# Post-norm attention with routed experts on one core: the transposed z moved between two projections, weight rounding and four orders moved

## The reference

```python
q, k, v = x@Wq + bq, x@Wk + bk, x@Wv + bv          # 16 heads of 64
attn = softmax(causal(q k^T / 8)); a = (attn v) @ Wo + bo
x = layernorm(x + a)
xn = layernorm(x) * gamma + beta
w, idx = top_k(softmax(xn @ router^T / 1.5), 2)    # 8 experts
y = sum_k w_k * (silu(xn @ W1[idx_k]) @ W2[idx_k])  # hidden 512
x = layernorm(x + y)
```

## Time and profile before

| | |
|---|---|
| median of 3 runs | 1347.1 us (1345.36 to 1347.86) |
| the profiled execution: time, span | 1345.8 us, 1344.0 us |
| TensorE, matmul | 1297.7 us busy, 97% |
| VectorE | 1116.6 us, 83% |
| ScalarE | 1037.2 us, 77% |
| GpSimd | 491.7 us, 37% |
| steps of attention | until about 1021 us |
| expert steps | until about 1296 us |
| last stage | until 1344 us |

### The profile page before, as it was taken

One profiled execution on the slowest core, in us unless ns is written; L12 is line 12 of the kernel. 1 busy time (PEld: TensorE's weight loads), 2 busy tenths in 40 slices (PEclk: granted clock), 3 DMA queues, 4 the chain that ended last, 5 costly groups with the idle time before them and its releaser, 6 DMA issues.

```text
span 1344.0 us, 35085 instructions
## 1 busy us (share of the span) xinstructions
PE 1297.7 (97%) x10918; PEld 1134.5 (84%) x10918; DVE 1116.6 (83%) x5412; ACT 1037.2 (77%) x3402; POOL 491.7 (37%) x1067
## 2 busy tenths in 40 slices
PE   6999999999999999999999999999998999999967
PEld 5888888888888888888888888888887999999953
DVE  6888888888888888888888888888886898888847
ACT  7888888888888888888888888888884555555527
POOL 1023333333333333333333333333335665555545
PEclk9999999999999999999999999999999999999989
DMA  2000000000000000000000000000033777666638
GB/s 82 2 5 17 16 16 19 13 14 13 14 13 13 14 14 14 13 14 18 16 18 15 14 13 14 13 14 14 14 140 114 216 221 219 213 214 209 205 123 327
DMA packets 67641, 89.74 MB, mean 67 GB/s; under 512 B 10352, under 2 KB 37107, under 8 KB 67456
## 3 DMA queue, kind: packets, MB, share of 16 engines
q1 hardware_dynamic: 57808, 70.28, 16.6%
q0 software_dynamic: 8640, 17.13, 3.8%
q10 hardware_dynamic: 1008, 0.08, 0.1%
HBM read 61.66 MB, written 26.71 MB: 66 GB/s over the span
## 4 chain that ended last, share of the span: by engine, by line
PE 93%; ACT 2%; DVE 2%; issue 1%; DMA 1%; POOL 0%; ACTq 0%; POOLq 0%; SPq 0%; DVEq 0%
PE ps_f L1036 15%; PE ps_b L1070 14%; PE ps_a L1036 13%; PE ps_s L1077 12%; PE ps_s L1058 10%; PE ps_s L1235 9%; PE ps_b L1244 5%; PE ps_a L1244 5%; PE ps_s L1061 4%; PE ps_s L1311 2%; PE ps_a L1226 1%; ACT probs L574 1%; PE ps_f L1102 1%; PE ps_s L1082 1%; ACT probs L576 1%
## 5 line engine op out<-in xcount | busy, mean ns | idle before, releaser
L574 ACT ACTIVATE probs<-probs,neg_max 128x256 f32<-128x256 f32 x512 | 255.3, 499 | 127.8 <-DVE neg_max L790 125.4
L786 DVE CUSTOM_DVE_ANT_0 probs<-ps_s,mask 128x256 f32<-128x256 f32 x512 | 214.4, 419 | 37.1 <-PE ps_s L1061 34.3
L450 POOL TENSOR_SCALAR ln_b<-mv 128x2 f32<-128x2 f32 x32 | 6.1, 190 | 637.4 <-DVE mv L853 637.4
L1070 PE MATMUL ps_b<-pt,f_y 128*64 128x256 f32 (+1 forms) x2048 | 196.0, 333 | 10.3 <-ACT f_y L569 7.3
L660 ACT ACTIVATE m_tanh<-ps_s 128x256 f32<-128x256 f32 x284 | 108.8, 384 | 124.7 <-PE ps_s L1235 114.8
L1077 PE MATMUL ps_s<-ident,probs 128*128 128x128 f32 x1536 | 204.7, 274 | 0.0
L576 ACT ACTIVATE probs<-probs,neg_max 128x128 f32<-128x128 f32 x512 | 198.7, 388 | 0.0
L800 DVE TENSOR_SCALAR probs<-probs,inv_sums 128x256 f32<-128x256 f32 x512 | 180.8, 353 | 9.1
L1070 PEld LDWEIGHTS ps_b<-pt,f_y 128*64 128x64 f32 x2048 | 132.0, 137 | 61.0 <-issue 16.3
L540 POOL DMA_INDIRECT y_tok<-m_y,m_dest x142 | 139.7, 984 | 111.5 <-DVE m_dest L946 79.4
L1058 PE MATMUL ps_s<-qk 64*128 64x256 f32 x1024 | 171.3, 408 | 7.9 <-ACT pt L605 1.7
(11 more groups left out here) (193 smaller groups left out, 2988.5 us busy)
## 6 DMA issues: line engine op xcount, KB each, us to landing
m_w<-in_w SPq DMA_DIRECT2D x142, 256.0 KB
m_x<-queue SPq DMA_DIRECT2D x71, 133.0 KB, 3.0
f_y<-y_tok SPq DMA_DIRECT2D x32, 256.0 KB, 6.5
queue<-empty SPq DMA_DIRECT2D x8, 532.0 KB, 5.0
x_raw<-in_x SPq DMA_DIRECT2D x32, 128.0 KB, 2.1
out_x<-f_y SPq DMA_DIRECT2D x16, 256.0 KB, 5.7
y_tok<-m_y,m_dest POOLq DMA_INDIRECT x142
queue<-z,slot_now POOLq DMA_INDIRECT x128, 2.4
```

Of the source, the lines that this page charges most:

```text
L574: act.activation(row[:, 0:2 * P], row[:, 0:2 * P], ACT.Exp, scale=-1.0, bias=neg_max[:, pair, h, 0:1], accum_out=sums[:, d % 2, pair, h, 0:1])
L786: dve.tensor_tensor_reduce(out=row[:, 0:2 * P], in0=ps_s[:, pair, h, 0:2 * P], in1=mask[:].rearrange("p a b -> p (a b)"), scale=-1.0, scal ...
L1070: ins = pe.matmul(ps_b[r, cols], v[:, k, c * P + h * DH:c * P + (h + 1) * DH], pt[:, pair, h, src], start=(k == 0), stop=(k == 1), skip_gr ...
```

## The change

The text of the change, with some unchanged lines left out:

```diff
@@ ScalarE, the start
-            for half in range(2):
+            def round_weights(half, i):
                 cols = slice(half * 512, (half + 1) * 512)
-                for i in range(3):
-                    act.wait_ge(attn_w_loaded[half * 3 + i], 16)
-                    act.activation(wqkv_hi[:, i, cols], wqkv_raw[:, i, cols], ACT.Copy, scale=SCALE if i == 0 else 1.0
-                                   ).then_inc(attn_w_hi, 1)
+                act.wait_ge(attn_w_loaded[half * 3 + i], 16)
+                act.activation(wqkv_hi[:, i, cols], wqkv_raw[:, i, cols], ACT.Copy, scale=SCALE if i == 0 else 1.0
+                               ).then_inc(attn_w_hi, 1)
+
+            for i in range(3):
+                round_weights(0, i)
             act.wait_ge(small_loaded, 16 * 7)
             act.wait_ge(biases_ready, 1)
             evacuate_qk(0, 0)
             evacuate_qk(0, 1)
+            for i in range(3):
+                round_weights(1, i)
@@ ScalarE, a step
+                if q == 3 and n in MID:
+                    act.wait_ge(zt_ready, n)
+                    act.activation(xnt[:].rearrange("p (i t) -> p i t", i=TILES), ps_s[:, 1, :, 3 * P:4 * P],
+                                   ACT.Identity, scale=gamma_sb[:, 0:1], bias=beta_sb[:, 0:1]).then_inc(xnt_done, 1)
                 if d >= 2 and q == 0:
                     copy_outputs(d)
                 if d + 1 < LAST:
                     evacuate_qk(d + 1, 0)
-                if q == 3 and n in MID:
-                    act.wait_ge(zt_ready, n)
                 if 1 <= d <= LAST:
                     first_pt(d)
-                if q == 3 and n in MID:
-                    act.activation(xnt[:].rearrange("p (i t) -> p i t", i=TILES), ps_s[:, 0, :, 3 * P:4 * P],
-                                   ACT.Identity, scale=gamma_sb[:, 0:1], bias=beta_sb[:, 0:1]).then_inc(xnt_done, 1)
@@ VectorE, the start
             rest_of_weights(0, 2)
-            for i in range(3):
-                rest_of_weights(1, i)
@@ VectorE, first_table: parts 4, 5, 6, 7 are now parts 3, 4, 5, 6
@@ VectorE, a step
-                if n == SEQS - 1 and q == 3:
-                    first_table(7)
...
                 if q == 0 and n < SEQS:
                     evacuate_first_v(n * 4 + 1, 0)
+                if d == 0:
+                    rest_of_weights(1, 0)
+                    rest_of_weights(1, 1)
+                if d == 1:
+                    rest_of_weights(1, 2)
                 if q == (3 if n < SEQS - 1 else 1):
                     evacuate_first_v(n * 4 + 3, 1)
+                if d == LAST - 1:
+                    second_pt(d)
                 if d < LAST:
                     normalise(d, 1)
-                if d >= 1:
+                if 1 <= d < LAST - 1:
                     second_pt(d)
@@ VectorE, an expert step
-                if j >= 2:
+                if 2 <= j < NJ - 1:
                     rows(j - 2)
+                if j >= NJ - 2:
+                    rows(j - 1)
                 keep(j)
...
-            rows(NJ - 2)
             rows(NJ - 1)
@@ TensorE, a step
-                        if pair == 0 and q == 0 and n >= 2:
-                            pe.wait_ge(xnt_done, n - 1)
...
-                    for pair in range(2):
-                        qk_projection((d + 1) // QUADS % 2, (d + 1) % QUADS * 2 + pair, pair)
+                    qk_projection((d + 1) // QUADS % 2, (d + 1) % QUADS * 2, 0)
+                if q == 3 and n in MID:
+                    pe.wait_ge(z_done, n)
+                    pe.wait_ge(max_done, d * 4 + 4)
+                    for i in range(TILES):
+                        ins = pe.transpose(ps_s[:, 1, i, 3 * P:4 * P], z[:, (n - 1) % 2, i, 0:D], ident[:])
+                    ins.then_inc(zt_ready, 1)
+                if d + 1 < LAST:
+                    qk_projection((d + 1) // QUADS % 2, (d + 1) % QUADS * 2 + 1, 1)
                 if 1 <= d <= LAST:
                     pe.wait_ge(probs_done, d * 2 - 1)
                     pe.wait_ge(max_done, min(d * 4 + 2, LAST * 4))
                     transpose_probs((d - 1) % 2, 0).then_inc(pt_first_ready, 1)
-                if q == 3 and n in MID:
-                    pe.wait_ge(z_done, n)
-                    for i in range(TILES):
-                        ins = pe.transpose(ps_s[:, 0, i, 3 * P:4 * P], z[:, (n - 1) % 2, i, 0:D], ident[:])
-                    ins.then_inc(zt_ready, 1)
                 if 1 <= d <= LAST:
                     pe.wait_ge(max_done, min(d * 4 + 4, LAST * 4))
+                if q == 3 and n in MID:
+                    pe.wait_ge(xnt_done, n)
@@ TensorE, expert step 1: the waits for r_diff_done, chosen_any_done, res_done and ranks(SEQS)
@@ now stand behind output(j - 1), not before it
```

18 lines of the change are left out of this document (9 added, 9 removed).

## The result

| | before | after |
|---|---|---|
| median | 1346.68 us (1345.36 to 1347.86, 4 runs) | 1331.46 us (1329.87 to 1332.10, 4 runs) |
| the profiled execution: time, span | 1345.8, 1344.0 us | 1330.95, 1329.2 us |

The ratio is 0.9885 (95% interval 0.9868 to 0.9903), 15.2 us less. The forecast was 12.0 less: 1335.1 us, with a range from 1331.5 to 1340.5, so the result lies 0.04 us under the range's lower end. In a later group, on one chip with other runs of before, the same two kernels gave 1331.82 and 1345.97: 0.9889 (0.9868 to 0.9910). At the slow site of the experiments some executions of before and of most variants took 1418 to 1425 us and all others 1388 to 1396; the ratios are of the others.

A forecast was written before the change was run, and what follows sets the result against it. With TensorE busy 1297.7 of 1344.0 us, only its gaps could move the end. Terms -9.9 - 0.5 + 0.3 - 0.7 - 1.2 = -12.0 gave 1333.8, plus 1.3 to the median: 1335.1 us, range 1331.5 to 1340.5.

The forecast's parts named there:

- Part 1: Changes of sequence: z transposed between the two projections, so v's copy comes 0.33 us earlier in 30 sequences, -9.9 us.
- TensorE's pace: Attention products after the last step's wait: ten took 1.98 us, elsewhere sixteen take 1.52; bound 2.0 if pace is kept.
- part 4: Start: weight halves moved behind ScalarE's first copies, two given to VectorE: +0.3 us, bounds -0.3 and +0.9.
- part 5: First expert steps: ranks behind the first expert's output, whose products fill TensorE's 0.73 us wait: -0.7 us, bounds 0 and -1.0.
- Rivals A: Sequences: a new wait for xnt or the first probabilities takes half the hole, 5.0 instead of 9.9, 1340.0 us; chance 0.12.
- B: Sequences: another ScalarE instruction releases v late, so only the ends count, -2.1, 1345.0 us; chance 0.07.
- C: Sequences: GpSimd delivers z 1.5 us later, TensorE stands 0.97 in each of 31 sequences, 1375 us; chance 0.03.
- 418.19: Sequence 13: when TensorE could start the attention products without any wait, 417.44 + 0.75; v was to free them then too.
- part 2: VectorE, last quarters: first experts' table one part earlier, VectorE and ScalarE about 0.6 earlier; -0.5 us together with part 3.
- part 3: VectorE, last step: second copy before the last normalising, at 1016.92 instead of 1017.42; -0.5 us together with part 2.
- Rival D: Last step: if TensorE's pace stays up, 1.5 us more comes off, 1333.6 us; chance 0.78 together with the forecast.
- part 6: Program end: expert rows made one step earlier, leaving 0.30 of GpSimd's 1.46 us wait before its sends: -1.2 us.

The follow-up runs named there:

- z_alone: Kernel before with only z transposed between the two projections and xnt made ahead of the first copies: 1334.23 us against 1346.12, ratio 0.9911.
- ends_alone: Kernel before with only the ranks behind the first expert's output and the last expert rows one step earlier: 1343.47 us against 1346.12, ratio 0.9976.
- after_again: The changed kernel run again, nothing altered, for a second trace at the usual site: 1331.82 us.
- table_undone_2: Changed kernel with the first experts' table back in its old places, at the slow site: lowest times 1392.78 and 1393.09 us, too few for a ratio.
- before_again: The kernel before run again, nothing altered, for a second trace at the usual site: 1346.39 us.

## Why the prediction was right or wrong

**What failed, in short.** The mechanism was right; two terms of the sum were too small, and a third number was off. Part 1 was put at -9.9 with "not below -9.9" and measured -10.99. TensorE's pace behind the last wait was put at 0 and measured -1.35 in the two traces. And 1.3 was added for the distance from the trace to the median, which was 0.5 for the changed kernel. That is 1.1 + 1.35 + 0.8 of the 3.6 us between 1335.1 and 1331.46; the other parts make up 0.4. The range's lower end had room for the pace, for parts 4 and 5 and for scatter, and none for more from part 1.

**The cause of the main gain was right.** The hole of 0.33 us behind z's transposes was what made v late. With it gone the 30 waits for v shrank to 0.1 each and z_alone has the whole gain. Rivals A, B and C fell: no new wait for z, xnt or the first probabilities appears in the sequences.

**Its size was wrong by 1.1 us, and the bound was wrong.** The forecast said "not below -9.9, since v can't come earlier than its chain". On average over 30 sequences the time from the last exponential of quarter 3 to v's copy fell from 3.774 to 3.431, which is 0.34, and that from the copy's start to the attention products from 0.886 to 0.860, another 0.03. The bound took the chain only as far as v's copy: the products follow the copy a little sooner when they have hardly waited. 30 times 0.366 is 10.98. The two numbers that had come out equal were 0.33 each from one sequence; 30 of them would have given 0.34, and the release had not been counted at all.

Something else had been put at nothing, and was needed for the last part. Before, the first scores of the next sequence waited for xnt at each of the 30 changes; they started 0.70 us behind its start. Freed of that, they start 5.990 us behind the products of quarter 3 instead of 6.145, and the second pair's scores 0.13 earlier too. With the second pair's scores where they were, TensorE's own distance of 0.75 would have ended the gain at 1.094 - 0.75 = 0.344 a sequence, or 10.3 in all (an estimate from these means). The "418.19" that the forecast had for TensorE was a second bound, and it moved.

**TensorE's pace was left at the wrong end of its range.** For parts 2 and 3 the forecast took 0.5 from "0 if ScalarE's chain doesn't move, and 2.0 if TensorE also keeps its pace". Rival D said that "1.5 more comes off" if it does. In the two traces it did, 1.35 us, and that with part 1's 1.1 makes up nearly all of the 2.8 us between -12.0 and -14.84. But what D called the change's doing is at least partly chance, and that these two traces had it so was luck. ends_alone has the gain without any of its causes, and after_again lost it again. In the medians, where before carries falls of up to 3.4 us, some of it stays. I can't say how much: the highest run of the changed kernel is 3.0 above its lowest (8 runs), that of before in one group 5.8 (13 runs).

**Parts 2 and 3** were 0.7 instead of 0.5, and all of it was part 2: VectorE's operations in front of the ranks' copy (0.73 us of waiting on TensorE in step 127, in before as in table_undone_2). The forecast had sized them at 0.6, and then took the gain at the copy of part 3, which turned out to move nothing. In before the normalising did hold the copy up, to 1017.42. But with part 1 the transposes that the copy waits for stand behind xnt, and the normalising ends in time for them. The forecast's own numbers had that: 0.6 from part 2 puts the end of the normalising at 1017.42 - 0.6 = 1016.82, in front of the 1016.92 worked out for the copy.

**Part 4** was within what the landing of the inputs and TensorE's clock at the start vary. **Part 5** gave 0.85 for 0.7, **part 6** 1.15 for 1.2, as worked out from the earlier trace rows, and ends_alone has both.

**The medians.** The trace of before lay 0.9 under its median of 1346.68 (1.3 under the 1347.1 that the forecast had), that of the changed kernel 0.5, so the medians differ by 15.2 where the traces differ by 14.84.

## What to carry to other kernels

A gap that recurs is best sized from all its instances, start to start and through to the instruction that is released, and after an operation has been moved off a chain one should look at the end of the chain again: here v's copy was still the last link, and giving it to the other engine took the remaining 0.10 us of each sequence. A "can't be more than" that comes from one instance is no bound. Where TensorE, otherwise busy, stands still as it does here (2.96 us whole, or three pieces of 0.75 to 1.28), its clock may or may not fall afterwards; the profile of one execution shows one outcome only, so such a term belongs in the range with both ends, and some useless transposes in the gap are a cheap way to take it out.

## What the runs showed of the hardware that had not been expected

- Behind the same 2.96 us of waiting TensorE's granted clock was 0.52, 0.53 or 1.00 in different executions; the stretch from the last step's attention products to the next ones took 6.37, 8.39 and 6.54 us in three traces of before, and 5.02 in ends_alone.
- Three waits of 1.18, 0.93 and 1.28 with short work between them were followed by the same fall (z_alone), three of 1.17, 0.75 and 1.28 by none (the first trace of the changed kernel).
- At the start, too, the clock differs between executions: in 7 of 13 traces at the usual site it was at half for some 3 us from about 18 us on (0.51 in 18 to 20 us in before_again, 1.00 in ends_alone), and step 7 then started some 1.0 us later than in the three traces with an equally early bias and a full clock.
- The kernel before takes 3.5% longer at one site than at the other, and variants of the changed kernel that should gain about 1.1% on it gained 0.0 to 0.2% there.
- ScalarE's copy of v and the products that wait for it start 0.89 us apart on average where the products have been waiting and 0.86 where they hardly wait; xnt and the scores that it held up start 0.70 apart, in all 30 sequences of before.
